# Row maxima two banks at a time, and begun by twos and fours, in an attention and coupling kernel

## The reference

```python
x = x + layernorm(attention(layernorm(x)))
x = x + layernorm(coupling(layernorm(x)))

def attention(x):                       # left 128 features, 16 heads of 8
    q, k, v = (left @ W.T for W in (Wq, Wk, Wv))
    att = softmax(q k^T / 4)            # 1024 x 1024 for each head
    return (att @ v) @ Wo.T + bo

def coupling(x):                        # three cycles
    gf = global_net(mean of x over the tokens)
    for _ in range(3):
        tf = sigmoid(gelu(gelu(gelu(x w1 + b1) w2 + b2) w3 + b3) w4 + b4)
        x = x + (0.1 + r * (0.7 gf + 0.3 tf - 0.5) * 2) * twist(x)
```

## Time and profile before

| | us |
|---|---|
| median of 3 runs | 3399.02 (3393.05 to 3400.91) |
| span of the profiled execution | 3391.6 |
| TensorE busy | 3222.9 (95%) |
| VectorE busy | 2992.7 (88%) |
| ScalarE busy | 2843.6 (84%) |
| GpSimd busy | 897.6 (26%) |

### The profile page before, as it was taken

One profiled execution on the slowest core, in us unless ns is written; L12 is line 12 of the kernel. 1 busy time (PEld: TensorE's weight loads), 2 busy tenths in 40 slices (PEclk: granted clock), 3 DMA queues, 4 the chain that ended last, 5 costly groups with the idle time before them and its releaser, 6 DMA issues.

```text
span 3391.6 us, 56526 instructions
## 1 busy us (share of the span) xinstructions
PE 3222.9 (95%) x19712; PEld 941.5 (28%) x19712; DVE 2992.7 (88%) x5577; ACT 2843.6 (84%) x3752; POOL 897.6 (26%) x1322
## 2 busy tenths in 40 slices
PE   6989999999999999999999999999999999999987
PEld 2222232322323232232322323232232322323223
DVE  7999989999898998989989898998989989898943
ACT  3868979798897979979798897979979798896975
POOL 5002050321505123050320505123050320504015
PEclk7998999999999999999999999999999999999999
DMA  3111111121111112121121111112121121111001
GB/s 90 26 41 43 32 50 33 44 50 44 50 31 51 43 39 55 33 61 32 44 49 44 50 31 51 42 39 55 33 61 32 45 49 44 38 32 51 8 22 38
DMA packets 97498, 144.75 MB, mean 43 GB/s; under 512 B 49472, under 2 KB 60096, under 8 KB 89408
## 3 DMA queue, kind: packets, MB, share of 16 engines
q1 hardware_dynamic: 93520, 123.83, 13.8%
q0 software_dynamic: 3696, 17.31, 2.8%
HBM read 34.61 MB, written 32.51 MB: 20 GB/s over the span
## 4 chain that ended last, share of the span: by engine, by line
PE 67%; DVE 17%; ACT 8%; issue 3%; SPq 2%; DMA 1%; POOL 1%; DVEq 0%; POOLq 0%; ACTq 0%
PE heads_ps L514 24%; PE ring_ps L481 15%; DVE max_parts L966 12%; PE scoresT_ps L499 11%; PE scoresT_ps L602 7%; ACT p_sb L719 4%; DVE stats L977 3%; PE scoresT_ps L607 2%; ACT headsT L728 1%; PE ring_ps L543 1%; SPq L346 1%; DVE state L1030 1%; ACT state L784 1%; DVE moments L987 1%; PE ring_ps L529 1%
## 5 line engine op out<-in xcount | busy, mean ns | idle before, releaser
L966 DVE TENSOR_REDUCE max_parts<-ring_ps 128x1 f32<-128x512 f32 x3744 | 2369.2, 683 | 225.4 <-PE ring_ps L481 166.3
L719 ACT ACTIVATE p_sb<-scoresT_ps 128x1024 f32<-128x1024 f32 x2048 | 1970.1, 1024 | 81.4 <-PE scoresT_ps L499 57.7
L481 PE MATMUL ring_ps<-k_rows,q_rows 48*128 48x512 bf16 x3744 | 1086.0, 384 | 33.1 <-DVE max_parts L966 23.8
L514 PE MATMUL heads_ps<-p_sb,v_sb 128*9 128x512 f32 x8192 | 1071.4, 595 | 17.9 <-ACT headsT L728 11.9
L499 PE MATMUL scoresT_ps<-q_rows,k_rows 51*128 51x512 bf16 x4096 | 1021.3, 383 | 7.1 <-ACT p_sb L719 4.3
L481 PEld LDWEIGHTS ring_ps<-k_rows,q_rows 48*128 48x128 bf16 x3744 | 265.5, 94 | 1353.4 <-DVE max_parts L966 1242.4
L1233 POOL CAST max_wide<-max_all 128x16 bf16<-128x16 f32 x128 | 25.4, 198 | 1743.0 <-DVE max_all L972 1743.0
L602 PE MATMUL scoresT_ps<-state,w 128*128 128x512 f32 x732 | 364.9, 621 | 13.3 <-DVE state L1030 12.3
L824 ACT ACTIVATE p_sb<-scoresT_ps,b 128x512 f32<-128x512 f32 x180 | 123.8, 688 | 194.2 <-PE scoresT_ps L602 193.2
L499 PEld LDWEIGHTS scoresT_ps<-q_rows,k_rows 51*128 51x128 bf16 x4096 | 207.0, 93 | 224.4 <-ACT p_sb L719 211.5
L514 PEld LDWEIGHTS heads_ps<-p_sb,v_sb 128*9 128x9 f32 x8192 | 124.4, 88 | 288.8 <-issue 278.3
(11 more groups left out here) (196 smaller groups left out, 2635.9 us busy)
## 6 DMA issues: line engine op xcount, KB each, us to landing
q_rows<-parts SPq DMA_DIRECT2D x744, 32.0 KB
k_rows<-parts SPq DMA_DIRECT2D x744, 32.0 KB
x_sb<-in_x SPq DMA_DIRECT2D x16, 1024.0 KB, 4.8
x_in<-in_x SPq DMA_DIRECT2D x15, 1024.0 KB, 5.4
out<-x_sb SPq DMA_DIRECT2D x15, 1024.0 KB, 3.9
out<-x_in POOLq DMA_DIRECT2D x15, 1024.0 KB, 7.9
q_rows<-max_rows SPq DMA_DIRECT2D x512, 3.0 KB
feat_h<-headsT SPq DMA_DIRECT2D x512, 16.0 KB
```

The lines of the kernel that those rows point to most:

```text
L481: e.matmul(ring_bank(max_taken, u + 1), q_rows[rows, slot, pair, h * BANK + qb * P:h * BANK + (qb + 1) * P], k_rows[rows, slot, pair, kh * ...
L514: m = e.matmul(heads_ps[32 * j:32 * j + DH + 1, :], v_sb[:, b % 2, kb, 4 * (group % NG) + j, 0:DH + 1], p_sb[:, n % 2, j, :], start=(kb == ...
L719: e.activation(p_sb[:, n % 2, 2 * two:2 * two + 2, :].rearrange("p h n -> p (h n)"), scoresT_ps[:, (2 - 2 * two) * BANK:(4 - 2 * two) * BA ...
L966: e.tensor_reduce(max_parts[:, gi % 2, kh, col:col + 1], bank_of(max_taken, u + 1), AX.X, ALU.max).then_inc(max_taken, 1)
```

## The change

`BEAT_UNITS` gets new numbers: 0, 2 or 4 units in each beat. TensorE hands out banks for two units at a time, if two more units are to be made at this place and two neighbouring banks are among the three that were handed out longest ago (`oldest_pair`); VectorE then reduces both banks by one instruction of 128x1024 to two columns, which waits for both matmuls and gives both banks back at its end. For the neighbourhood all eight banks become one tensor: ring 0 to 2, heads 3, scores 4 to 7, and the spare bank of the scores is its first, so that the order of the layers' banks and that of the two score pairs are mirrored. `max_parts` is laid out by unit and the join reads it with another pattern. A unit's release is now counted by instruction (`taken_by`) instead of by unit.

```diff
-BEAT_UNITS = (4, 1, 2, 1, 2, 1, 2, 2, 1, 1,
-              2, 3, 2, 3, 3, 2, 2, 4, 2, 1,
-              2, 1, 2, 3, 4, 2, 2, 2, 3, 1)
+BEAT_UNITS = (4, 0, 2, 2, 0, 2, 2, 2, 0, 2,
+              2, 2, 4, 2, 2, 4, 2, 4, 2, 0,
+              2, 2, 2, 4, 2, 4, 2, 2, 2, 2)
...
+        all_ps = ctx.enter_context(nc.psum_tensor("all_ps", [P, 8 * BANK], F32))
+        ring_ps = all_ps[:, 0:RING * BANK]
+        heads_ps = all_ps[:, RING * BANK:(RING + 1) * BANK]
+        scoresT_ps = all_ps[:, (RING + 1) * BANK:]
...
+        starts = [i * BANK for i in (*range(RING), RING + 1, RING)]
+        banks = [all_ps[:, at:at + BANK] for at in starts]
...
+        def units_banks(u, size):
+            ends = [starts[unit_bank[v]] for v in (u, u + size - 1)]
+            both = all_ps[:, min(ends):max(ends) + BANK].rearrange("p (k n) -> p k n", n=BANK)
+            return both[:, ::-1, :] if ends[0] > ends[1] else both
...
+                u, upto = done, min(upto, N * UNITS)
+                while u < upto:
+                    pair = oldest_pair() if u + 1 < upto else ()
+                    size = 2 if pair else 1
+                    first_of.append(u)
+                    for v in range(u, u + size):
+                        taken_by[v] = len(first_of)
+                        max_unit(v, pair[v - u:v - u + 1])
+                    u += size
+
+            def oldest_pair():
+                oldest = sorted(range(ring[0]), key=lambda k: turn[k])[:3]
+                pairs = [(i, j) for i, j in itertools.permutations(oldest, 2) if starts[j] - starts[i] == BANK]
+                return min(pairs, key=lambda ij: max(turn[ij[0]], turn[ij[1]])) if pairs else ()
...
+            def max_pack(u, size):
+                for v in range(u, u + size):
+                    gi = v // PER_GROUP
+                    e.wait_ge(max_done[v % 2], v // 2 + 1)
+                    if v % PER_GROUP == 0 and gi >= 2:
+                        e.wait_ge(max_joined, gi - 1)
+                at, last = u % (2 * PER_GROUP), (u + size - 1) % (2 * PER_GROUP)
+                out = max_parts[:, last:at + 1][:, ::last - at] if last < at else max_parts[:, at:last + 1]
+                e.tensor_reduce(out, units_banks(u, size), AX.X, ALU.max).then_inc(max_taken, 1)
```

More of the change, by code:

```diff
@@ L145, in attention_ffn_program @@
         warm = sb("warm", [P, 1])
[L146 removed]
+        max_parts = sb("max_parts", [P, 2 * PER_GROUP])
         max_all = sb("max_all", [P, MU])
@@ L456, in spare_banks, with ring_bank @@
                         turn[i], freed[i] = next(turns), last
-            def ring_bank(evacuated, count, rest=0):
-                i = min(range(ring[0]), key=lambda k: turn[k])
+            def ring_bank(evacuated, count, rest=0, i=None):
+                if i is None:
+                    i = min(range(ring[0]), key=lambda k: turn[k])
                 if freed[i]:
@@ L470, in max_units, with max_unit @@
             def max_units(done, upto):
[L471 to L475, removed]
+                u, upto = done, min(upto, N * UNITS)
[11 more added lines that the diff above has]
+                return min(pairs, key=lambda ij: max(turn[ij[0]], turn[ij[1]])) if pairs else ()
+            def max_unit(u, bank=()):
                 b, h, g, two, qb, kh, side = unit_place(u)
@@ L480, in max_unit @@
                     e.wait_ge(pool_laid[g], 12 * 16)
-                e.matmul(ring_bank(max_taken, u + 1),
+                ps = ring_bank(max_taken, taken_by[u], 0, *bank)
+                unit_bank[u] = place[max_taken.name, taken_by[u]]
+                e.matmul(ps,
                          q_rows[rows, slot, pair, h * BANK + qb * P:h * BANK + (qb + 1) * P],
@@ L954, in max_units @@
             def max_units(done, upto):
[L955 to L963, removed]
-                    e.wait_ge(max_joined, gi - 1)
-                col = (side * 2 + two) * TPH + qb
-                e.tensor_reduce(max_parts[:, gi % 2, kh, col:col + 1], bank_of(max_taken, u + 1),
-                                AX.X, ALU.max).then_inc(max_taken, 1)
-                if (u + 1) % PER_GROUP == 0:
-                    e.wait_ge(max_taken, u + 1)
-                    if gi:
-                        e.wait_ge(max_cut, gi)
-                    e.tensor_tensor(max_all[:, :], max_parts[:, gi % 2, 0, :], max_parts[:, gi % 2, 1, :],
-                                    ALU.max).then_inc(max_joined, 1)
+                u = done
@@ new lines, in max_units @@
+                while u < min(upto, N * UNITS):
+                    first, size = pack_of(u)
+                    max_pack(first, size)
+                    u = first + size
+            def max_pack(u, size):
[7 more added lines that the diff above has]
+                e.tensor_reduce(out, units_banks(u, size), AX.X, ALU.max).then_inc(max_taken, 1)
+                for v in range(u, u + size):
+                    if (v + 1) % PER_GROUP == 0:
+                        join(v // PER_GROUP)
```

29 lines of the change are left out of this document (20 added, 9 removed).

## The result

The changed kernel takes 3445.4 us (median of 4 runs, 3444.1 to 3448.8) against 3398.6 (4 runs, 3393.1 to 3400.9) on the same chip: ratio 1.0144, 95% interval 1.0129 to 1.0158. That is 1.4% slower. Forecast was no difference (3404, range 3384 to 3420), so the forecast was wrong, in size and in kind. Two executions among the experiments, of 4931.6 and 14511.3 us, stand far apart from all others and are left out of the times.

A forecast was written before the change was run, and what follows sets the result against it. Bounds taken: ScalarE's exponentials in steady attentions, VectorE in the first attention, TensorE busiest in couplings. 3391.6 + 21.0 - 14.3 - 1.5 = 3396.8 us of span; with 7.4 to the median, 3404.2 us; range 3384 to 3420.

The forecast's parts named there:

- The order of banks in the first attention and its price: First attention: in 32 of 64 steps the pair waits for the reduction issued just before; 21 us more, bounds 15 and 26.
- The steady attentions: Steady attentions: the wait for a pair is hidden by the exponential that the second scores wait for; 0 us.
- The lead at project_out: Couplings up to project_out: TensorE let in after the division at 1447.50, a gain of 1.16 us; 0 in batches 4, 5, 14.
- the couplings, -14.3 forecast: Couplings of batches 1 to 14: 1.27 us gained in eleven, 0.11 in three, 14.3 us in all; bounds 0 and 35.
- Beats 10 to 19 are set by VectorE ... 0: Coupling, beats 10 to 19: one unit more (0.60 us) against ten pairs (0.50) on VectorE; no change.
- Beats 20 to 29 ... +0.33: Coupling, beats 20 to 29: fewer second slots, two small waits less, one more; 0.33 us gained.
- Rival (c): Couplings: pairs free only as a whole, new waits at beats 6, 7, 15, 16, 18 eat the gain; 3420 us, 27%.
- So it can't begin before 1441.52: Couplings: the reciprocal, 1.37 us after SyncE's last issue (1440.15), can't begin before 1441.52, where it began at 1442.47.
- ahead of the first attention: Before the first attention: 60 units form 27 pairs, each saving VectorE 0.05 us; about 1.5 us gained, at least 0.
- The unit groups: Couplings: TensorE's groups of units take 9.4 us in place of 11.3, so 1.9 us of TensorE saved.
- the first coupling: First coupling, without layers: 21 pairs less three waits of 0.5 us, taken to cost nothing.
- The term of 7.4 us between span and median: Whole kernel: the median of the runs lies 7.4 us above the profiled execution's span, added to the forecast span.

## Why the prediction was wrong, point by point

**Right.** What bounds each stage. The length of a pair (1.214 us for 1.23, 1.14 held for 1.15). The pairs' number. The order of banks in the first attention and its price (19.4 for 21), shown by the experiments with and without it (180.8 us with after's banks whatever the reduction, 161.1 to 162.3 without them). The steady attentions, which did not move (129.98 for 129.96). The lead at project_out in a coupling where the transfer lands early (1.24 for 1.16), at beat 7 and at beat 10 (0.81 and 0.93, as the terms add up).

The Trainium skill, page VectorE: DVE Perf Modes, section on the TRN2 errata, would have a pair save 0.125 us by its fixed 120 cycles, an estimate from its figure. The record saves a little more (2 x 0.689 - 1.214 = 0.16 us), but VectorE's pitch in a stream only 0.06: the measured value that the sum used stands.

**Wrong: the couplings, -14.3 forecast, +23.0 measured.** 37.3 of the 45.6 us that are missing in the sum lie here. Up to project_out the couplings gained 6.7 us where 12.8 were forecast: 6.1 short. From there on they lost 29.7 where 1.5 were to be gained: 31.2 more, of which 8.4 are falls of the clock and 22.8 waits. Three steps failed.

The first and largest is "Beats 10 to 19 are set by VectorE ... 0" and "Beats 20 to 29 ... +0.33". I had added up group slots and let each wait of before stay as it was. The runs show 1.55 us lost from project_out on in a clean coupling, where the terms had 0.11 of gain, and by the table above most of it is new waits for banks: 0.53 come with the new numbers alone, where four units follow one another (beats 12, 15, 17, 23, 25), 0.84 with the order of banks and only 0.18 with the wide instruction. The same order that the prediction walked bank by bank in the first attention, and priced within 2 us, it put at nothing in the coupling. Rival (c) had new waits at beats 15 and 16, with 27%, but laid them to the pair that is only free as a whole, the smallest of the three here, and let them eat only the gain. With the old numbers that cause is the larger one (1.53 of the 1.96 us that the pairs alone lose there).

The second is "So it can't begin before 1441.52". This was the time of coupling 6, taken for eleven. The rule behind it was right: 1.37 us after SyncE's last issue. But the issue has its own time in every coupling, and those times stood in the trace of before, whether the transfer was waited for or not. Put through the same steps they give the eleven couplings some 8 us in place of 12.8 (an estimate from SyncE's rows); in coupling 9 the reciprocal waited already, by 0.10 us. The rest is that SyncE issues 0.3 to 0.7 us later in couplings 3, 4, 5 and 9 of the kernel after. The experiment with project_out one beat later gets back 20.8 us, more than this step cost, so it acts on other waits as well.

The third is not a step but a gap: the granted clock isn't in the prediction at all, except as a column in the earlier trace rows that said 1.00. It went with some 13 us after (8.4 in couplings, 4.4 in attentions 1 and 12). Not all of that need come from the change: attention 1 took 133.0 us with the new numbers alone too, but 130.4 with after's banks and single reductions, and the kernel before was profiled in its fastest execution. I took "TensorE has less to do" for free. No run shows that it is: all twelve variants with a usable profile ran at a lower mean clock in it (0.977 to 0.982, against 0.985 in the kernel before; the pairs alone are without falls in couplings 1 to 13), and the same kernel's runs line up along it. The new numbers alone took 3403.7 us at a mean clock of 0.983, 3409.9 at 0.981 and 3416.2 at 0.978. Yet a lower mean clock does not make a kernel the slower one: the new numbers with the later project_out beat the kernel before at 0.978 to 0.982. The Trainium skill has the shape of it: TensorE: Matmul & The Clock Gate, section on psum-queue depth-cycling, tells of short idles of TensorE between groups of matmuls as it cycles through banks, by which the clock goes back and forth, the cost being paid between bursts. The traces here agree in part: behind some waits for a bank of 0.47 to 1.18 us 1.3 to 1.6 us were lost, but the kernel before waits 1.0 us for a bank in each of couplings 2 to 13 and its clock did not fall there.

**Wrong, small:** ahead of the first attention, +2.4 for -1.5 (and 27 x 0.05 is 1.35). VectorE ran there from 31.3 to 58.6 us without an idle time and was taken to gain 0.05 a pair; with pairs it waits 0.79, 1.09 and 1.15 us for TensorE. The order of banks is the likely cause, not a shown one: kernels with after's banks reach the first scores at 72.9 to 74.2 us, those without at 71.4 to 72.8. The unit groups were to free 1.9 us of TensorE and freed 1.26. And the first coupling, +1.8 for 0: the new numbers alone and the steady pairs alone took 56.8 us there, at a lower mean clock (0.63 for 0.68), but the kernel after had 0.72, so the clock is not what made it longer, and its cause is open. The term of 7.4 us between span and median holds the same accident as above: in the kernel after it is 3.0.

The sum: 6.1 + 22.8 us in couplings, 12.8 of clock, 5.7 at the start and in the first coupling, -1.6 in the first attention, 45.8 in all, against 50.8 - 5.2 = 45.6. The 22.8 are what is left when the rest is taken off; 1.66 x 14 = 23.2 from a clean coupling agrees with them.

**Open.** What decides that the clock falls at one of two places with the same waits. Filling the empty beats moved the falls and did not settle it. And why the wide instruction costs 1.5 us a coupling with the old numbers and 0.2 with the new, and after's order of banks more with the new: the waits are there in the traces, but I have no reason that would have given these numbers ahead.

## What to carry to other kernels

An instruction that serves two buffers is paid for in which buffers it needs and when they come free, not in its own length; walk the buffers turn by turn in every stage where they are scarce, not only in the one that looks tightest. A transfer that no one waits for in the old trace still has its issue there: before moving a consumer earlier, read that issue in every stage and add the time from issue to use that a stage with a wait shows. And see whether the consumer can be moved with it, as the later project_out did, which turned the new numbers from 0.5% slower into 0.15% faster. And look at the clock in more than one execution: a single profile can hold the best one.

## What the runs showed of the hardware

The granted clock fell for single stretches within stages where TensorE is busy 92 to 95% of the time, each behind or within a wait of TensorE of 0.3 to 2.9 us (the longest in coupling 4 of the new numbers alone), and cost 1.0 to 1.7 us each; the one in attention 1, with more of it at the lower level, went with 2.8. The same waits were also followed by no fall elsewhere. In an attention that is bound by ScalarE it cost just as much (131.44 for 129.87), although one would think ScalarE's exponentials hide a slower TensorE. A mean clock lower by 0.001 went with 2.1 to 3.1 us more in the runs of one kernel (3403.7, 3409.9, 3416.2 us at 0.983, 0.981, 0.978).

From the end of SyncE's last issue of the heads' transfer to the reciprocal that waits for it 1.36 or 1.37 us passed in thirteen of the fourteen full couplings of the kernel after.

A reduction over two banks costs VectorE 1.14 us in a stream. Three of them in a row, from the kernel after:

```profile
1536.64 3.49 DVE L999 TENSOR_REDUCE max_parts<-all_ps 128x2 f32<-128x1024 f32 x3 [1.01 <-PE all_ps L511]
```
